# Layer 0 of a two-layer network: dense experts to gathered rows, split scores to rounded 64-row products, a slot grid to one written-out order

## The reference, cut to what matters

```
# 16 heads of 16 dimensions, key blocks of 32 tokens, 4 blocks chosen per query
q, k = rope(xn @ Wq.T), rope(xn @ Wk.T);  v = xn @ Wv.T
gate = einsum('bshd,bnhd->bhsn', q, mean_of_blocks(k))     # future blocks -1e30, own block +1e30
sel  = top 4 blocks of gate per query and head
p    = softmax(where(sel & causal, q @ k * d**-0.5, -1e30))
o    = p @ v;  o = o * rsqrt(mean(o*o) + 1e-6) * o_norm_w;  s = o @ Wo.T
# 8 experts of width 176, 2 per token, and one shared expert of width 352
scores = softmax(xn @ gate_w);  comb = the two largest scores, else 0
g = einsum('teh,ehd,te->td', silu(x@w_gate)*(x@w_up), w_down, comb) \
  + silu(x@sw_gate)*(x@sw_up) @ sw_down
```

## Time and profile before

| | |
|---|---|
| median of the runs shown | 425.53 us |
| the profiled execution, its own time | 424.22 us |
| its span, first to last instruction | 422.4 us |
| PE busy | 348.9 us, 83% |
| DVE busy | 300.3 us, 71% |
| POOL busy | 172.9 us, 41% |
| ACT busy | 170.7 us, 40% |
| mean granted TensorE clock | 0.935 of full |
| DMA moved | 30.2 MB, 71 GB/s over the span |

### The profile page before, as it was taken

How to read it: one execution, slowest core, us unless ns; L and a number is a source line. 1 busy time by engine, 2 the same in 40 slices (tenths; PEclk the granted TensorE clock), 3 DMA queues, 4 the chain that set the end, 5 groups by cost and what they waited for, 6 DMA issues and landing times. The chain is left out here.

```text
span 422.4 us, 6057 instructions
## 1 busy us (share of the span) xinstructions
PE 348.9 (83%) x2028; PEld 240.3 (57%) x2028; DVE 300.3 (71%) x857; ACT 170.7 (40%) x305; POOL 172.9 (41%) x119
## 2 busy tenths in 40 slices
PE   0697767668779989999999999999682888996881
PEld 0586555546546657676665665656581776444641
DVE  3867489867997877894444764684668859758794
ACT  1422453551224323226444445544212475956610
POOL 5654283473444642554256526664536000000023
PEclk9999689697999999999999999999966789999898
DMA  8300168987793311212211141110006100000011
GB/s 267 74 23 21 50 160 178 163 141 182 183 180 88 87 47 44 70 37 52 63 43 42 40 137 39 39 37 2 1 2 216 48 0 2 0 1 0 2 50 50
DMA packets 17009, 30.20 MB, mean 71 GB/s; under 512 B 3140, under 2 KB 12012, under 8 KB 16556
## 3 DMA queue, kind: packets, MB, share of 16 engines
q1 hardware_dynamic: 12946, 18.80, 19.2%
q10 hardware_dynamic: 4032, 11.01, 9.0%
HBM read 24.99 MB, written 4.82 MB: 71 GB/s over the span
## 5 line engine op out<-in xcount | busy, mean ns | idle before, releaser
L388 POOL TENSOR_TENSOR wl<-wr,wh 128x768 fp32r<-128x768 f32 x28 | 51.2, 1829 | 65.3 <-ACT wh L474 49.1
L530 ACT ACTIVATE PT<-bank 128x512 f32<-128x512 f32 (+1 forms) x88 | 44.3, 557 | 39.5 <-PE bank L952 39.4
L687 DVE TENSOR_REDUCE mx<-bank 128x1 f32<-128x384 f32 (+3 forms) x88 | 52.2, 635 | 7.2 <-PE bank L934 6.9
L149 PE MATMUL bank<-xh,wh 128*128 128x512 f32 x112 | 50.7, 452 | 4.0 <-DVE gb L812 1.4
L426 POOL TENSOR_TENSOR gl<-gb,gh 128x512 fp32r<-128x512 f32 x28 | 36.5, 1302 | 37.5 <-DVE gh L819 24.9
L151 PE MATMUL bank<-xh,wl 128*128 128x512 f32 x112 | 45.7, 408 | 0.0
L150 PE MATMUL bank<-xl,wh 128*128 128x512 f32 x112 | 45.5, 407 | 0.0
L933 PE MATMUL bank<-KS,QS 112*128 112x128 bf16 (+3 forms) x128 | 32.9, 310 | 12.5 <-DVE mx L687 6.8
L1213 POOL TENSOR_TENSOR left<-xn,x 128x256 f32<-128x256 f32 x8 | 7.0, 898 | 85.1 <-DVE xn L1440 85.1
L149 PE MATMUL bank<-wh,gh 128*128 128x256 f32 x112 | 36.9, 329 | 0.5 <-POOL gl L426 0.5
L537 ACT ACTIVATE th<-bank 128x512 f32<-128x512 f32 x28 | 16.7, 597 | 45.9 <-PE bank L151 45.8
(11 more groups left out here) (233 smaller groups left out, 824.7 us busy)
## 6 DMA issues: line engine op xcount, KB each, us to landing
wr<-in_w_chunks_dram ACTq DMA_DIRECT2D x28, 384.0 KB, 3.1
KS<-parts_dram SPq DMA_DIRECT2D x12, 256.0 KB, 8.0
parts_dram<-wp SPq DMA_DIRECT2D x12, 128.0 KB
QS<-parts_dram SPq DMA_DIRECT2D x2, 768.0 KB
parts_dram<-x SPq DMA_DIRECT2D x12, 128.0 KB
w_ai<-in_w_ai_dram SPq DMA_DIRECT2D x1, 1152.0 KB, 6.6
x<-in_x_dram SPq DMA_DIRECT2D x2, 512.0 KB, 6.6
QS<-parts_dram SPq DMA_DIRECT2D x2, 512.0 KB
```

What stands on the lines that cost most here:

```text
L149: pe.matmul(out, l_hi, r_hi, start=start, stop=False, skip_group_check=skip)
L388: pool.tensor_tensor(wl[:, s % 3, :, :], wr[:, s % 2, :, :], wh[:, s % 3, :, :].bitcast(F32), ALU.subtract).then_inc(wl_ready, 1)
L530: act.activation(PT[:, k % 8, 0:n], bank[k % 2][:, 0:n], ACT.Exp, scale=float(DH) ** -0.5).then_inc(P_ready, 1)
L687: dve.tensor_reduce(mx[:, b * TB + i, heads[0]:heads[-1] + 1], bank[k % 2][:, 0:len(heads) * n].rearrange("p (h n) -> p h n", n=n), AX.X, ...
```

## The change

Layer 0 is written anew; layer 1, and the first layer norm's arithmetic, stay. The slot grid goes. In its place `program_order` writes out one list of items, `ORDER`, and every engine walks it and does its part of each item. `weave` merges lists by the share of their cost done. Its beginning is: QK0-3 RO0 RO1 RK RO2 KT RO3 KT KT SG KT KM0 QK4 RO4 KT SG QK5 RO5 KT SEL QT GT SG QT GT QT GT SD SEL QK6 RO6 KT SEL SEL QK7 SD RO7 KT KM1. Then the list has 7 QT, 32 SA, 3 SEL with choices, 3 SG, 3 GT, 2 SD; then 8 QT, 32 SA, 32 SB, 16 PV, 14 row tiles; then 4 QT, 32 SB, 16 PV and the other row tiles; then GA, MZ, WO.

- **QK, RO, KT, QT**: projection of a tile, rotation, and on-chip transposes of rows `[hi, lo, hi, bias]` of 4 x 16 for two heads side by side, so that one rounded product of 64 rows makes q k with its low parts and the block bias. No parts go through DRAM. QT is made three times (for the gates, the maxima, the exponentials).
- **SA, SB**: scores of two heads, in rows 0-63 and 64-127 of the array, into two of four banks. All of KT, QT, GT, SA, SB, RS, RT, WO, RK share a ring of two places: PE may fill a place once the item two before has been read by its engine.
- **RK, M1 to M4, GA, MZ**: the two chosen experts of each token give it two places among 23 tiles of 128 rows (`NT`), sorted by expert. POOL scatters xn to `xg_dram` with 16 indirect DMAs. Each tile loads its expert's weights at an address read from `eid`, is transposed (M1), multiplied in plain f32 (M2), transposed (M3) and multiplied (M4), and its rows go to `yg_dram`. 16 indirect DMAs gather them, and DVE adds them with the routing weights (MZ).
- **SG, SD**: the shared expert, 6 and 4 items. Its second product, and the one with Wo (WO), are plain f32.

```diff
+            chunks = a["w_chunks"]                                   # SP
+            for k in range(KD):
+                for side in range(2):
+                    sp.dma_start(wide_dram[2 * k + side].rearrange("p (c n) -> p c n", n=P),
+                                 chunks[0:ECH, :, k, side * P:(side + 1) * P].rearrange("c p n -> p c n")
+                                 ).then_inc(relaid, 16)
+            sp.dma_start(down_dram.rearrange("(c p) d -> c p d", p=P), chunks[0:ECH, :, KD, :]).then_inc(relaid, 16)
+            sp.wait_ge(zero_ready, 1)
+            sp.dma_start(xg_dram.rearrange("(j p) d -> p j d", p=P), spread(ysb[:, 0, :], 1, NT)).then_inc(cleared, 16)
...
+                if kind == "RO":                                     # POOL
+                    t = item[1]
+                    pool.wait_ge(qk_read, t + 1)
+                    pool.tensor_tensor(rot_a[:, t % 2, :], rot_a[:, t % 2, :], rot_b[:, t % 2, :],
+                                       ALU.add).then_inc(sum_ready, 1)
+                    pool.wait_ge(sum_ready, t + 1)
+                    pool.wait_ge(hi_ready, t + 1)
...
+                    pool.tensor_tensor(q[:, :, 2 * DH:3 * DH], r[:, 0], q[:, :, 0:DH], ALU.subtract)
+                    pool.tensor_tensor(Zk[:, t % 2, :, DH:2 * DH], r[:, 1], Zk[:, t % 2, :, 0:DH],
+                                       ALU.subtract).then_inc(lo_ready, 1)
+                    if t == TB - 1:
+                        pool.wait_ge(slots_ready, 1)
+                        pool.wait_ge(cleared, 16)
+                        pool.wait_ge(xn_dve, T // 2)
+                        pool.wait_ge(xn_act, T // 2)
+                        for t in range(T):
+                            for k in range(2):
+                                pool.indirect_dma_start(xg_dram, bass.IndirectOffsetOnAxis(ap=slots[:, t, k:k + 1], axis=0),
+                                                        xn[:, t, :], None).then_inc(scattered, 16)
...
+                if kind == "GA":
+                    t = item[1]
+                    if t == 0:
+                        for k in range(2):
+                            pool.wait_ge(y_out[k], 16 * ((NT + 1 - k) // 2))
...
+                    for k in range(2):
+                        pool.indirect_dma_start(yg[:, t, k, :], None, yg_dram,
+                                                bass.IndirectOffsetOnAxis(ap=slots[:, t, k:k + 1], axis=0)
+                                                ).then_inc(gathered[t // TB], 16)
...
+                if kind == "RO":                                     # ACT
...
+                    act.copy(Zk[:, t % 2, :, 3 * DH:ROW], spread(onehot[:, t % TB, :], 1, H))
+                    act.copy(q.bitcast(F32R), spread(r[:, 0], 2, 2))
+                    act.copy(k[:, :, 0:3:2, :].bitcast(F32R), spread(r[:, 1], 2, 2)).then_inc(hi_ready, 1)
...
+                if kind == "SA":                                     # PE
+                    b, i, p = item[1:]
+                    n = (i + 1) * P
+                    wait_read(pe, ("QT", b, i, 1))
+                    wait_read(pe, ("KT", b, i))
+                    ring_wait(item)
...
+                    for h in range(2):
+                        rows = slice(ROW * h, ROW * (h + 1))
+                        pe.matmul(out[:, h, 0:n], qA[rows, (b * TB + i) % 2, p, :], kT[b][rows, p, 0:n], start=True, stop=False)
+                    for h in range(2):
+                        ins = pe.matmul(out[:, h, n - P:n], ident_b[:, :], tri[:, 0, :], start=False, stop=True)
+                    ins.then_inc(ring_ready, 1)
...
+                if kind == "M2":
+                    j = item[1]
+                    pe.wait_ge(w_in[j % 3], 16 * (j // 3 + 1))
+                    pe.wait_ge(xgT_read, j + 1)
+                    if j:
+                        pe.wait_ge(mg_ready, j)
+                    for k in range(KD):
+                        ins = pe.matmul(GUb[:, 0:GU], xgT[:, j % 2, k * P:(k + 1) * P], w_gu[:, j % 3, k * GU:(k + 1) * GU],
+                                        start=(k == 0), stop=(k == KD - 1))
+                    ins.then_inc(GU_ready, 1)
```

More of the change, by code:

```diff
@@ L62 @@
 OW = N_SEL * H_SEL + N_SEL
[L65 to L111, removed]
 def spread(ap, axis, n):
@@ L151, in split_matmul, with weave, cost @@
     return pe.matmul(out, l_lo, r_hi, start=False, stop=stop, skip_group_check=skip)
+NT = (T * P * EK) // P + E - 1
+GU = 2 * EH
+NP = H // 2
+ROW = 4 * DH
+E2 = EH - P
+RING_ENGINE = {"RK": "dve", "KT": "act", "QT": "act", "GT": "act", "SA": "dve", "SB": "act", "RS": "dve", "RT": "dve",
+               "WO": "dve"}
+def weave(first, second):
+    def cost(item):
+        return ITEM_COST.get(item[0], 0.0)
+    total = [sum(cost(i) for i in s) for s in (first, second)]
+    done, at, out = [0.0, 0.0], [0, 0], []
+    while at[0] < len(first) or at[1] < len(second):
+        if at[1] >= len(second) or (at[0] < len(first) and done[0] / total[0] <= done[1] / total[1]):
+            k = 0
+        else:
+            k = 1
+        item = (first, second)[k][at[k]]
+        out.append(item)
+        done[k] += cost(item)
+        at[k] += 1
+    return out
@@ L154, in layer0 @@
+ORDER = program_order()
+RING = [i for i in ORDER if i[0] in RING_ENGINE]
+RING_AT = {i: k for k, i in enumerate(RING)}
+RING_READ = {}
+for _i in RING:
+    RING_READ[_i] = 1 + sum(RING_ENGINE[_j[0]] == RING_ENGINE[_i[0]] for _j in RING_READ)
+CHUNKS = [i[1:] for i in ORDER if i[0] == "SB"]
+GATE_TILES = [i[1:] for i in ORDER if i[0] == "GT"]
+CHUNK_AT = {c: k for k, c in enumerate(CHUNKS)}
 def layer0(nc, a, x1, cst):
@@ new lines, in layer0, with overlay @@
+        mhalf = m.sb("mhalf", [P, TB * HG])
+        x = xn = x1
+        V = m.sb("V", [P, T, H, 32])
+        def overlay(early, late):
+            first = ExitStack()
+            a = [Mem(nc, first).sb(*t) for t in early]
+            first.close()
+            b = [m.sb(*t) for t in late]
+            size = [sum(int(np.prod(t[1][1:])) for t in ts) for ts in (early, late)]
+            if size[0] > size[1]:
+                m.sb("gap_" + late[-1][0], [P, size[0] - size[1]])
+            return a + b
@@ L437, in _ @@
-            if OUT_SLOT[-1] + 1 >= STEPS * SLOTS:
-                inverse_roots(B * NG - 1)
-            pool.wait_ge(x_again, 16)
-            pool.wait_ge(onT_ready, 2 * B)
-            for n in range(T // 2):
-                pair = slice(2 * n, 2 * n + 2)
-                pool.wait_ge(gated_ready, n + 1)
-                pool.tensor_tensor(x1[:, pair, :], xr[:, pair, :], y[:, pair, :], ALU.add)
+            pool.memset(mg[:, :, EH:2 * P], 0.0).then_inc(pads_init, 1)
+            pool.memset(gates[:, :, :, NBLK:GATE_ROW], SENT).then_inc(pads_init, 1)
```

1500 lines of the change are left out of this document (754 added, 746 removed).

## The result

The changed kernel takes **541.13 us** (median; 540.96 and 541.31 in two runs) against 425.53: 1.273 times as long, 95% interval 1.266 to 1.279. It is slower, as forecast, but by 116 us and not by 52, and outside the range. The profiled execution took 541.31 us, 1.7 more than its span. Some executions take some per cent longer at a lower granted clock; the figures of an experiment leave such runs out unless it says otherwise.

The account below looks back on a forecast made before the run. TensorE was taken to bound layer 0, its work falling from 270 to 219 us but POOL's queue leaving it idle. Head 140, stages 57, 86, 53 and tail 36 gave X = 372; plus 106.6, 478.6 us, said as 478; range 408 to 518.

Parts of the forecast that it names:

- X: Time at which layer 1 starts: 318.9 us before, forecast 372; the kernel's time is this plus 106.6 us.
- head: Layer 0 before the first scores: POOL's 16 scatters, 21 us, hold batch 1's rotations; scores start at 140 us.
- first stage: Maxima of batch 0 and choices of batch 1, held by VectorE, 10 us of TensorE work leaking: 57 us, to 197.
- tail: Last row tile to layer 1: 16 gathers on POOL, 21 us, then landing, combining and additions; 36 us.
- the last line of the forecast: In the head: if the cleared buffer lands before 50 us, 15 us go at once.
- about 54: In the head, from RO 4 to the first scores: rotations, choices, keys and means, about 54 us not hidden by anything.
- Per pair of heads 0.23/0.175/0.12/0.12 if both run at once, and two masks of 0.06: 128 pairs, 36 us: TensorE's score products, made twice in layer 0: both heads multiply at once, 36 us of the 219 us sum.
- surcharge of 18: Score pairs on TensorE: if the two heads run one after the other, 18 us more, part hidden on VectorE.
- Some 15 us more in head and stage 1: Lower TensorE clock in the head and first stage, some 15 us, counted within the main case and its range.
- Second and third stage: Score passes with row tiles: TensorE's 77 and 50 us of work, with hand-overs 86 and 53 us.
- Cheap and dear indirect DMAs: Rivals on POOL's scatters and gathers: cheap at 0.44 us, time 421, chance 0.12; dear at 3.1 us, 530, chance 0.11.
- The faster case: Rival: the head overlaps as well as the middle, 51 us less TensorE work; scores at 80, time 390; chance 0.15.

## Why the prediction was wrong

The sign and its chain were right, the size was not: 64 us of X. Stage by stage, forecast and measured: head 140 and 136.7; first stage 57 and 82.8; second 86 and 100.4; third 53 and 68.6; tail 36 and 47.5.

1. **The head** was right in its parts: scatters at 1.3 us (1.27), TensorE waiting at tile 4 (22.45 us), scores at 140 (136.7). The buffer landed before 50 and not at 65, 15 us early, as the last line of the forecast provided for. They did not come off the end, since "about 54" from RO 4 to the scores was 71.2 to 136.7, 65.5: a tile's chain takes 10 to 13 us where I had put 6 and "part beside". Two errors of 15 and 11 cancelled, so that the head came out within 3 us is luck.
2. **"Per pair of heads 0.23/0.175/0.12/0.12 if both run at once, and two masks of 0.06: 128 pairs, 36 us"** is the term that failed most. In the last two stages, start to start over the timeline, the products of 96 pairs took 36.1 us and their masks 17.2, at a clock of 0.95: 0.53 a pair at the full clock, so 68 for 128 and 32 us too few. I had the right answer to "at once or not" and missed the 0.21 us at the passage to half the rows. My surcharge of 18 for heads one after the other bounded the wrong thing. "For row groups no row shows it" was true of two halves at once, not of the passage: the kernel before has a product of 64 rows (`ksel`) between full-height ones.

```profile
201.08 0.40 PE L150 MATMUL bank<-xl,wh 128*128 128x512 f32 x1
201.31 0.40 PE L151 MATMUL bank<-xh,wl 128*128 128x512 f32 x1
201.64 0.39 PE L1013 MATMUL bank<-combT,ksel 64*128 64x512 bf16 x1
201.96 0.23 PE L951 MATMUL bank<-QS,KS 115*128 115x128 bf16 x1
```

The first three have 512 columns. The product of 64 rows starts 0.33 us behind the one ahead of it and is followed after 0.32, where full-height ones are 0.23 apart: 0.2 us at a passage, to be read before the change. (The 0.32 stands between two bf16 products, so it is not the change of type.)
3. Smaller terms of the sum, from the same distances at the full clock: transposed blocks 1.0 us and not 0.86 (30: +4), gate products 1.5 to 2 and not 1.0 (6: +4), root sums and their transposes 1.4 a group and not 0.9 (+4), row tiles 2.7 to 2.8 and not 2.6 (+4). With the pairs that is some 48 of the 50. (I had set the 219 against 270 us of busy time, which holds 10.5 of lower clock; against 259.6 the saving forecast was 41 and not 51.)
4. **The clock.** "Some 15 us more in head and stage 1" stood only in the range; it was 42 in layer 0, put at nothing in the sum. 15 of it lie in the head, where filler raised the clock and gained nothing, and 13.5 in the first stage. I gave that stage to VectorE (26 + 16.5 + 4 us of its work; it was busy for 46.5) and let 10 us of TensorE's work leak. TensorE was busy for 64.4 of 82.8 us there, at 0.79. Of the 26 us that the stage took more than forecast, 12 go when the row tiles go, 9 of them the wait for `mgT`; I had no row tile in this stage. How the rest divides between clock and work stays open. The kernel before had 0.90, 1.00 and 0.82; I carried the 1.00 of its middle to a kernel whose middle has other instructions.
5. **Second and third stage.** TensorE leads as forecast (92%), with 88 and 60 us of work, not 77 and 50. Waits came to 9% of the busy time in both, where I had put 12% and 6% for hand-overs, so it was the busy time that was wrong: the larger work and 8 us of lower clock.
6. **The tail**: the last row tile ended at 392.3, 3.7 us behind the cut, and the first gather was issued at 398.9, 6.6 us later and not 3, since it stood behind a power on POOL's queue; the gathers took 20.8 of 21. POOL's last additions took 4.6 us and not 2.6, and 2.9 pass from their end to layer 1, which had no term.
7. **Rivals.** Cheap and dear indirect DMAs are out (1.27 us apart, the longest of the 32 took 1.58). The faster case had the work of TensorE as its ground, 51 us less: it was 9 more. Packed and clocked as before, the true work would have given X = 269 + 10 + 49 = 328, still 9 later than before.

## What to carry to other kernels

- Price an instruction in the company that it will keep. A pair of half-height products between full-height ones costs its columns and 0.21 us, and up to 0.09 on the product ahead; four together cost the 0.21 once. By this, such products belong side by side, before a mask or any other full-height product; no kernel with its masks kept was built so.
- Work taken off TensorE is not time gained if the clock falls: compare busy time times granted clock with the time. If a stage is busy and its clock low, add harmless full-height products as a test; here 192 of them took 25 us off where the clock had been 0.6, 96 gave nothing where it had been 0.79 to 0.89, and 140 gave nothing where TensorE waited for others.
- In one list that all engines follow, look at what stands between two steps of one tile: a small copy behind three block choices cost 9 us. Writing a tile's last step behind the next tile's first should shorten the chain of the head, but it was not tried. Moving two things out of one hole pays once.

## What was not expected of the hardware

- With row tiles gone, TensorE, busy for 91% of 154 us with half-height scores, products of 32 output columns, transposes and masks, was granted 0.64 and 0.58 of its clock; no gap between its products was over 1.1 us but one of 3.9. With the same work and two full-height bf16 products before each pair it was granted 1.00 and 0.94.
- (The Trainium skill, "TensorE: Matmul & The Clock Gate", HAM oscillation — how this bites in real kernels, puts the low clock down to idle gaps of the engine. Here the measurement differs: these 154 us with few gaps had the lower clock, the kernel before had 0.90 over a stretch with TensorE busy for 69%, and full-height products added to the same work raised it. Whether their kind or their number did that no run separates, and what the clock follows stays open.)
- An indirect DMA of 128 rows of 1 KB takes POOL 0.95 or 0.96 us and 0.30 to the next; of the 32, six took 1.01 to 1.58. 16 plain transfers of the same size in place of the gathers took 14 us off.
